# Broadcasting the softmax normaliser once per pair of heads, and copying it out of PSUM on VectorE instead of ScalarE

## The reference

```python
xn = layernorm(x)                                   # no affine part
qkv = xn @ w_in.T ; q, k, v = split(qkv)            # 16 heads of 64
# sliding window: blocks of 512 queries, keys of the previous and the own block
scores = q @ k.T / 8 + slope[h] * (qi - kj + 512)   # valid where 0 <= qi - kj + 512 <= 512
p = softmax(scores) ; o = p @ v ; attn = o @ w_out.T
x_scale = max(|xn|) / 127 per token ; x_q = round(xn / x_scale)
ffn = (x_q @ weight_q.T) * x_scale * weight_scale + bias
out = x + attn + ffn
```

## Time and profile before

| what | value |
|---|---|
| median of 3 runs | 3258.06 us (3255.05 to 3258.15) |
| the profiled execution | 3256.65 us, span of its slowest core 3255.1 us |
| spans of the 8 cores | 3222.6 to 3255.1 us |
| granted TensorE clock, mean of a core | 0.720 to 0.726 |
| busy TensorE, ScalarE, VectorE | 74%, 52%, 43% of the span |

### The profile page before, as it was taken

How to read it: one execution, slowest core, us unless ns; L and a number is a source line. 1 busy time by engine, 2 the same in 40 slices (tenths; PEclk the granted TensorE clock), 3 DMA queues, 4 the chain that set the end, 5 groups by cost and what they waited for, 6 DMA issues and landing times.

```text
span 3255.1 us, 41352 instructions; the slowest of 8 cores (3222.6 to 3255.1 us)
## 1 busy us (share of the span) xinstructions
PE 2421.7 (74%) x10448; PEld 1041.6 (32%) x10560; DVE 1406.9 (43%) x3616; ACT 1687.7 (52%) x3969; POOL 141.8 (4%) x266
## 2 busy tenths in 40 slices
PE   0267779687795878778787777877778587877877
PEld 0123334233342423334233333423334232333433
DVE  0345344453443445434454443445434444443424
ACT  0154572745726275482754548275482627538274
POOL 0000000000000000000000000000000000000000
PEclk9977759567595956858568685866858686585867
DMA  7411202002020300202002020300202020020100
GB/s 149 102 62 38 71 7 104 4 32 77 6 104 6 105 4 20 88 7 105 4 20 89 19 91 7 105 3 18 91 7 104 6 81 28 11 97 6 67 3 31
DMA packets 63135, 160.97 MB, mean 49 GB/s; under 512 B 6722, under 2 KB 6978, under 8 KB 62530
## 3 DMA queue, kind: packets, MB, share of 16 engines
q1 hardware_dynamic: 46066, 105.88, 9.7%
q0 software_dynamic: 16848, 52.45, 5.5%
HBM read 119.51 MB, written 37.75 MB: 48 GB/s over the span
## 4 chain that ended last, share of the span: by engine, by line
PE 49%; DVE 12%; ACT 12%; DMA 11%; issue 7%; ACTq 6%; DVEq 3%; SPq 0%; POOLq 0%
PE ps L606 14%; PE ps L456 8%; ACT pe_buf L650 7%; PE ps L629 7%; PE ps L702 7%; PE ps L714 7%; ACTq L105 6%; DMA x_tm<-x 4%; DMA wqk<-w2bf 4%; PE ps L548 3%; DVEq L105 3%; ACT zln L530 2%; DVE stt L276 2%; DVE stt L278 2%; PE ps L410 1%
## 5 line engine op out<-in xcount | busy, mean ns | idle before, releaser
L650 ACT ACTIVATE pe_buf<-ps,ebias_sb 128x128 bf16<-128x128 f32 (+4 forms) x2560 | 905.6, 500 | 274.4 <-PE ps L629 271.5
L663 DVE TENSOR_TENSOR pe_buf<-pe_buf,tripo_sb 128x128 bf16<-128x128 bf16 x1792 | 381.3, 223 | 909.4 <-ACT pe_buf L650 858.4
L606 PE MATMUL ps<-pe_buf,v_st 128*65 128x128 bf16 (+3 forms) x2368 | 602.3, 404 | 157.4 <-DVE pe_buf L663 143.5
L629 PE MATMUL ps<-q_fm,k_st 64*128 64x512 bf16 (+3 forms) x1792 | 481.8, 419 | 273.0 <-ACT pe_buf L650 262.8
L456 PE MATMUL ps<-xn_fm,wqk 128*128 128x512 bf16 x2000 | 456.2, 380 | 54.7 <-DMA wqk<-w2bf 43.7
L606 PEld LDWEIGHTS ps<-pe_buf,v_st 128*65 128x65 bf16 x2368 | 294.5, 157 | 469.9 <-issue 393.7
L468 ACT CAST q_fm<-ps 128x512 bf16<-128x512 f32 x128 | 75.0, 586 | 618.3 <-PE ps L456 618.3
L629 PEld LDWEIGHTS ps<-q_fm,k_st 64*128 64x128 bf16 x1792 | 122.4, 101 | 609.8 <-issue 594.5
L456 PEld LDWEIGHTS ps<-xn_fm,wqk 128*128 128x128 bf16 x2048 | 195.1, 98 | 313.1 <-issue 92.7
L267 DVE BATCH_NORM_STATS2 stbn<-x_tm 128x6 f32<-128x512 f32 x64 | 43.6, 681 | 546.1 <-DMA x_tm<-x 546.1
L702 PE MATMUL ps<-wout_sb,o_fm 128*128 128x512 bf16 x992 | 252.5, 409 | 5.6 <-issue 3.7
(11 more groups left out here) (52 smaller groups left out, 1629.5 us busy)
## 6 DMA issues: line engine op xcount, KB each, us to landing
wqk<-w2bf SPq DMA_DIRECT2D x128, 512.0 KB, 4.0
x_tm<-x SPq DMA_DIRECT2D x16, 2048.0 KB, 8.5
out<-outhf POOLq DMA_DIRECT2D x128, 256.0 KB, 2.3
o_fm<-o_stage POOLq DMA_DIRECT2D x128, 64.0 KB, 1.9
k_st<-w POOLq DMA_DIRECT2D x2, 2048.0 KB, 17.0
w2bf<-k_st SPq DMA_DIRECT2D x2, 2048.0 KB
wv_sb<-wv POOLq DMA_DIRECT2D x1, 2048.0 KB, 18.6
wout_sb<-wout POOLq DMA_DIRECT2D x1, 2048.0 KB, 17.6
```

The lines of the kernel that those rows point to most:

```text
L606: slp=slp, first=pv_first[hh], lastp=lastp: e.matmul(out=psum[ob][0:65, c0:c0 + cw], lhsT=vsl, rhs=pe_buf[:, 512 * slp + (c0 - qsp):512 * ...
L629: qs=qs, w=w, ksl=ksl: e.matmul(out=psum[b][:, 0:w], lhsT=ksl, rhs=q_fm[base2:base2 + 64, pr2 * 512 + qs:pr2 * 512 + qs + w], start=True, ...
L650: sl_pe=sl_pe, ecol=ecol: e.activation(out=pe_buf[:, 512 * sl_pe + a0 - qs:512 * sl_pe + a1 - qs], in_=psum[b][:, a0 - qs:a1 - qs], func=A ...
L663: gm = P.op("vector", lambda e, sl_pe=sl_pe, tloc=tloc, tsel=tsel: e.tensor_tensor(out=pe_buf[:, 512 * sl_pe + tloc:512 * sl_pe + tloc + 128],
```

## The change

`flush_div_b` handles the two heads of a pair together:

- both spreading matmuls write one PSUM bank, head A on partitions 0 to 63 and head B on partitions 64 to 127 (`tile_position=(0, 64)`). The instruction before had the array divided into tiles of 32 rows and 64 columns as well, always with the tile at (0, 0);
- one copy of 128 partitions on VectorE takes the place of two copies of 64 partitions on ScalarE. It waits for both matmuls;
- the multiplication of head A reads partitions 0 to 63 of `zb_sb`, that of head B reads partitions 64 to 127 of it, with its PSUM operand and its output still on partitions 0 to 63;
- one bank fewer is taken and returned per pair;
- a constant `ones2` of 2x128 is loaded at the start, as one more link of the SyncE chain. No instruction reads it.

```diff
+        ones2_sb = sb("ones2_sb", [2, 128], BF16)
...
-        zb_sb = sb("zb_sb", [64, 1024], BF16)
+        zb_sb = sb("zb_sb", [128, 512], BF16)
...
-                         (ebias_sb[:, :], ebiash), (tripo_sb[:, :], tripoh), (ones_sb[:, :], onesh)]:
+                         (ebias_sb[:, :], ebiash), (tripo_sb[:, :], tripoh), (ones_sb[:, :], onesh),
+                         (ones2_sb[:, :], ones2h)]:
...
-                for (hh, ob, vz) in jobs:
...
-                    zbk, zbw = banks.acquire()
-                    tzb = P.op("tensor", lambda e, zbk=zbk, sl=sl: e.matmul(
-                        out=psum[zbk][0:64, :], lhsT=ones_sb[0:1, :],
-                        rhs=zr_sb[0:1, 512 * sl:512 * (sl + 1)],
-                        start=True, stop=True), waits=[("S", vz)] + zbw, inc="T")
-                    szb = P.op("scalar", lambda e, zbk=zbk, sl=sl: e.copy(
-                        out=zb_sb[:, 512 * sl:512 * (sl + 1)], in_=psum[zbk][0:64, :]),
-                        waits=[("T", tzb)] + zb_free[sl], inc="S")
-                    banks.release(zbk, [("S", szb)])
...
+                (hA, obA, vzA), (hB, obB, vzB) = jobs
+                pr = hA // 2
+                zbk, zbw = banks.acquire()
+                P.op("tensor", lambda e, zbk=zbk: e.matmul(
+                    out=psum[zbk][0:64, :], lhsT=ones_sb[0:1, :], rhs=zr_sb[0:1, 0:512],
+                    start=True, stop=True),
+                    waits=[("S", vzA)] + zbw, inc="T")
+                tzb = P.op("tensor", lambda e, zbk=zbk: e.matmul(
+                    out=psum[zbk][64:128, :], lhsT=ones_sb[0:1, :], rhs=zr_sb[0:1, 512:1024],
+                    start=True, stop=True, tile_position=(0, 64)),
+                    waits=[("S", vzB)], inc="T")
...
+                szb = P.op("vector", lambda e, zbk=zbk: e.tensor_copy(
+                    out=zb_sb[:, :], in_=psum[zbk][:, :]),
+                    waits=[("T", tzb)] + zb_free[0], inc="V")
+                banks.release(zbk, [("V", szb)])
...
+                vdo = P.op("vector", lambda e, obA=obA, d=dsto: e.tensor_tensor(
+                    out=d, in0=psum[obA][0:64, :], in1=zb_sb[0:64, :], op=ALU.mult),
+                    waits=[("V", szb), ("T", prevT)], inc="V")
...
+                vdo2 = P.op("vector", lambda e, obB=obB: e.tensor_tensor(
+                    out=o_stage[0:64, :], in0=psum[obB][0:64, :],
+                    in1=zb_sb[64:128, :], op=ALU.mult),
+                    waits=[("V", szb)] + ostg_free[0], inc="V")
```

More of the change, by code:

```diff
@@ L87, in _host_constants @@
     c["ones_bf"] = np.ones((1, 64), BF)
+    o2 = np.zeros((2, 128), BF)
+    o2[0, 0:64] = BF(1.0)
+    o2[1, 64:128] = BF(1.0)
+    c["ones2"] = o2
     return c
@@ L158, in build_nc @@
     onesh = nc.dram_tensor("ones_bf", [1, 64], BF16, kind="ExternalInput").ap()
+    ones2h = nc.dram_tensor("ones2", [2, 128], BF16, kind="ExternalInput").ap()
     w2bf = nc.dram_tensor("w2bf", [16, 128, 8, 128], BF16, kind="Internal").ap()
@@ L543, in flush_div_b @@
                 jobs = [divq2.pop(0) for _ in range(min(k, len(divq2)))]
-                for (hh, ob, vz) in jobs:
-                    sl = hh % 2
-                    pr = hh // 2
-                    zbk, zbw = banks.acquire()
-                    tzb = P.op("tensor", lambda e, zbk=zbk, sl=sl: e.matmul(
-                        out=psum[zbk][0:64, :], lhsT=ones_sb[0:1, :],
-                        rhs=zr_sb[0:1, 512 * sl:512 * (sl + 1)],
-                        start=True, stop=True), waits=[("S", vz)] + zbw, inc="T")
-                    zr_free[sl] = [("T", tzb)]
-                    szb = P.op("scalar", lambda e, zbk=zbk, sl=sl: e.copy(
-                        out=zb_sb[:, 512 * sl:512 * (sl + 1)], in_=psum[zbk][0:64, :]),
-                        waits=[("T", tzb)] + zb_free[sl], inc="S")
-                    banks.release(zbk, [("S", szb)])
[L557 to L577, removed]
@@ new lines, in flush_div_b @@
+                if not jobs:
+                    return
+                assert len(jobs) == 2 and jobs[0][0] % 2 == 0, [j[0] for j in jobs]
+                (hA, obA, vzA), (hB, obB, vzB) = jobs
[5 more added lines that the diff above has]
+                    waits=[("S", vzA)] + zbw, inc="T")
@@ new lines, in flush_div_b @@
+                tzb = P.op("tensor", lambda e, zbk=zbk: e.matmul(
+                    out=psum[zbk][64:128, :], lhsT=ones_sb[0:1, :], rhs=zr_sb[0:1, 512:1024],
+                    start=True, stop=True, tile_position=(0, 64)),
+                    waits=[("S", vzB)], inc="T")
+                zr_free[0] = [("T", tzb)]
+                zr_free[1] = [("T", tzb)]
+                szb = P.op("vector", lambda e, zbk=zbk: e.tensor_copy(
+                    out=zb_sb[:, :], in_=psum[zbk][:, :]),
+                    waits=[("T", tzb)] + zb_free[0], inc="V")
@@ new lines, in flush_div_b @@
+                banks.release(zbk, [("V", szb)])
+                dsto = o_fm[0:64, pr * 512:pr * 512 + 512]
+                vdo = P.op("vector", lambda e, obA=obA, d=dsto: e.tensor_tensor(
+                    out=d, in0=psum[obA][0:64, :], in1=zb_sb[0:64, :], op=ALU.mult),
+                    waits=[("V", szb), ("T", prevT)], inc="V")
+                banks.release(obA, [("V", vdo)])
+                ofm_by_pair[pr].append(("V", vdo))
+                vdo2 = P.op("vector", lambda e, obB=obB: e.tensor_tensor(
+                    out=o_stage[0:64, :], in0=psum[obB][0:64, :],
+                    in1=zb_sb[64:128, :], op=ALU.mult),
+                    waits=[("V", szb)] + ostg_free[0], inc="V")
@@ L579, in emit_attn @@
+                banks.release(obB, [("V", vdo2)])
+                zb_free[0] = [("V", vdo2)]
+                sh = dma("gpsimd", o_fm[64:128, pr * 512:pr * 512 + 512],
+                         o_stage[0:64, :], "SH0",
+                         waits=[("V", vdo2), ("T", prevT)])
+                ostg_free[0] = [("SH0", sh)]
+                ofm_by_pair[pr].append(("SH0", sh))
             for pr_grp in range(8):
@@ L798, in _shard_inputs @@
                   ident=consts["ident"], ebias=consts["ebias"],
-                  tri_post=consts["tri_post"], ones_bf=consts["ones_bf"])
+                  tri_post=consts["tri_post"], ones_bf=consts["ones_bf"],
+                  ones2=consts["ones2"])
     in_maps = []
```

## The result

The kernel with the change takes 3335.0 us in the median of its runs, against 3257.8 us for the kernel before in the same comparison: a ratio of 1.0227, with a 95% interval of 1.020 to 1.0253, so 74 us slower by the ratio. The profiled execution's slowest core has a span of 3339.3 us, 84 us more than before. The direction was forecast, the size was not: 3283 us was predicted, with a range up to 3312.

A forecast was written before the change was run, and what follows sets the result against it. TensorE and ScalarE were taken to bound attention by turns, with VectorE ending last after the change. Terms 2.5 + 11.2 + 12.3 + 0.5 = 26 us on the profiled 3256.65 us gave 3283 us, range 3252 to 3312.

The forecast's parts named there:

- What bounds the kernel: Attention: TensorE and ScalarE take turns; ScalarE's two copies, 1.06 us a pair, precede 1.60 of idle time, so removing them gains nothing.
- That margin: 8-chunk pair before the change: VectorE's second mask would let the last product start at 3.16, against 3.4, some 0.2 us spare.
- The hand-over of 0.15: Time from a VectorE instruction's end to TensorE's start, 0.15 us, applied between the second mask and the last product with v.
- The 8-chunk term: 84 flushes in 8-chunk pairs: next scores at 3.60 in place of 3.57, 0.03 later each, 2.5 us in all.
- The spreading matmuls: At a flush in 8-chunk pairs: the two run side by side on two column tiles, saving TensorE 0.42 us.
- the serial case: Rival: the two column tiles run one behind the other, +63 us, 3320 us; chance 0.16.
- The price of the copy: VectorE's new copy of 128x512 from PSUM to bf16 in SBUF takes 0.68 us, as L392 does.
- the short copy: Rival: VectorE's copy takes half of L392's time, 0.34 us, so the kernel gets faster, -32 us, 3225 us; chance 0.12.
- The lost overlap: VectorE: head B's operand at partition 64 and the return to partition 0 cost 0.07 us each, 0.14 per flush.
- The 4-chunk term: 28 flushes in 4-chunk pairs: packing saves nothing, the copy queues behind two masks, next scores 0.40 us later, 11 us.
- The end: 16 flushes behind the last pair of a block: VectorE's chain into the next tokens' scaling 0.77 us later, 12 us.
- The start: Loads at the kernel's start: the added link for `ones2` costs 0 to 1.8 us, taken as 0.5.

## Why the prediction was right and wrong

**What bounds the kernel.** That the two engines take turns, and that ScalarE's copies lie in front of idle time, was right: with them gone ScalarE's wait went from 1.60 to 2.81 us. The step that failed is the next one: "A hand-over from VectorE to TensorE takes 0.15 [...], so the mask would let it start at 3.16. VectorE is some 0.2 short of ending last. That margin decides the case." There was no such margin. One more VectorE instruction of 0.13 made each pair 0.13 longer, and with the masks out of the way the products needed 2.28 for the 2.36 of the earlier trace rows, so that the masks already ended last, by 0.08. The hand-over of 0.15 was read from a transpose, and it was set against the second mask and the last product. The rows of the place itself read otherwise. First the first of the two masks and TensorE's weight loads before, then the weight loads in the change, then those of the kernel with the masks first ("issue": the view names nothing that the engine waited for):

```profile
856.49 0.21 DVE L663 TENSOR_TENSOR pe_buf<-pe_buf,tripo_sb 128x128 bf16<-128x128 bf16 x1
856.91 0.36 PEld L606 LDWEIGHTS ps<-pe_buf,v_st 128*65 128x65 bf16 x2 [0.20 <-issue]
...
877.36 0.36 PEld L616 LDWEIGHTS ps<-pe_buf,v_st 128*65 128x65 bf16 x2 [1.05 <-issue]
...
851.78 0.60 PEld L623 LDWEIGHTS ps<-pe_buf,v_st 128*65 128x65 bf16 x3
```

The first mask ends at 856.69. The weight load of the seventh product starts 0.22 later and its matmul at 856.95, and from there the steps are 0.22 to the eighth product and 0.22 to the next scores. Where nothing waits, the eighth follows the seventh at 0.11 and the scores follow 0.25 later. From the end of the first mask to the next scores it is 0.70 in all seven kernels that keep the multiplications ahead of the masks, the kernel before among them, in the median of either kind of pair on the slowest core (0.702 to 0.704). In the change with the masks first it is 1.2 to 1.4: there the masks are early, and TensorE's own work decides.

The packed trace also holds the waits of TensorE's queue, which no view prints. Each of the last two products has two, one for VectorE's mask and one for ScalarE's exponential, 0.11 apart. With the masks first they are over more than 0.6 us ahead of their matmuls at the flush shown. Here those of the seventh product start at 856.73, 0.04 behind the first mask, and those of the eighth follow the seventh's weight load, though the second mask (over at 856.83) would have let them go 0.1 earlier. So the first mask gates the path, and what follows it is the queue working through waits and loads.

"There is no gap in this stretch" was the misreading: one row of eight products printed no gap, since the 0.29 to 0.31 that it gives for a product of 128 columns covers a slot of 0.11 and one of 0.22 alike.

**The 8-chunk term**, 2.5 us predicted, 36 measured, holds most of the miss. Per flush the next scores came at 4.00 in place of 3.60. Of these 0.40 us 0.23 are the way just told (from the end of the second mask to the next scores 0.58, reckoned as 0.15 + 0.2), and the masks' end at 3.42 in place of 3.25 is the other 0.17: the copy started at 0.84 and not at 0.78 (0.06), the copy and its hand-over took 0.02 more, and the lost overlap and the slightly longer masks are the rest. The first flush of a block lost 0.66 and not 0.42: there ScalarE is late with the exponentials of the steep heads, so that VectorE's masks ahead of the copy are late too, and the copy starts 1.09 after the spreading. That was not foreseen, 12 times 0.24, or 3 us.

**The spreading matmuls** side by side, 0.42 saved on TensorE: right, and the serial case is out. What the Trainium skill says of weight loads in one row group (page "TensorE: Matmul & The Clock Gate", Part 3) does not hold these two apart: they start 0.01 us from each other. The estimate from its speed-up of column tiles, 0.37 saved, is not borne out either: the products start 0.78 behind the spreading, in place of 1.21. **The price of the copy**, 0.68: 0.69 in 128 cases, the short copy is out. **The lost overlap**: right in kind, 0.10 to 0.12 instead of 0.07 a place, shown by the kernel in which head B reads partition 0. **The 4-chunk term**, 11 predicted and 21 measured, misses for the same reason: the next scores came 0.75 later and not 0.40, and of the missing 0.35 0.22 are the way from the masks to the scores and 0.13 a later end of the masks. **The end**, 12 predicted and 14 measured, is right within its parts: 0.89 for 0.77. **The start**: the added link cost nothing.

One gain was overlooked. With one bank fewer in use, the last scores of a 4-chunk pair no longer wait for a bank. In the kernel before, this row ran 0.60 for two matmuls that start apart, since the second waits for an exponential of ScalarE that frees its bank (over at 1004.80):

```profile
1004.61 0.60 PE L629 MATMUL ps<-q_fm,k_st 64*128 64x128 bf16 x2
```

In the change the same row has 0.29, side by side. It is worth 0.31 a pair only with the masks first (8.59 against 8.90).

## What to carry to other kernels

Work moved to an engine with much idle time is free only if nothing on the critical path stands behind it in that engine's list; measure the distance from the end of each such instruction to the next step of the path, in one piece, from the rows of the same place, and do not take a hand-over from another place. A gap that is not printed is no proof of slack: compare the stretch with the same instructions where they cannot wait, or put one small instruction in front and see whether the time moves. An edit that does nothing alone (the masks first, 0.9997) and a change that costs time alone (1.0227, or 1.0105 for its packing) were worth 1.3% together (0.9875), since one makes the room and the other clears the way.

## What was unexpected in the hardware

Products with v whose waits have just ended do not follow each other at the pace of the others. After a stall the last product started 0.23 behind the one before it and the scores 0.22 behind that, though the second mask ended only 0.13 behind the first; in the kernels with the masks first the two products were 0.11 apart at the same granted clock of 0.50. The records of TensorE's queue show why: two waits 0.11 apart and then the weight load, 0.23 from load to load. With the masks first those waits were over more than 0.6 us ahead and cost nothing. On VectorE the step over to an operand at partition 64 and the step back cost 0.10 and 0.12 us. A whole copy from one ScalarE instruction of 128 partitions or two of 64 made no difference to when the first of them could start, 0.78 to 0.81 after the spreading, but VectorE needed 0.84 for the same start. Of the two copies of 64 partitions out of one bank, the second from partition 64, the second started 0.60 behind the first and 0.02 after its end, where the two copies from two banks were 0.48 apart and overlapped; no run separates the bank from the partition.
